# A spectral stage's causal filters computed in two block levels with three products each, image by image

## The chip, the core and the metric

The kernel is one program on one core of a Trainium2 chip. The core's engines are TensorE (PE, matrix products from SBUF into PSUM), VectorE (DVE), ScalarE (ACT), GpSimd (POOL) and SyncE (SP), which issues the DMAs. Each engine runs its own instruction list; semaphores order them. The metric is the device time of one execution in microseconds; three runs of the kernel before gave 12062.67 to 12078.81, median 12070.78.

## The reference

A four-layer model on x of 2 images x 4096 tokens x 128 channels, float32. The change touches one part, the spectral feed-forward of layer 2:

```python
for i, frac in enumerate((1, 2, 4, 8)):
    xi = x[:, :T // frac]
    si = _stu(xi, sigma, phi, M_u[i], M_phi_plus[i], M_phi_minus[i])   # padded back to T tokens
    outs.append(si)
# _stu: for each of K = 16 filters phi[:, k] (4096 taps, causal):
#   U_plus  = conv(phi_k, u);  U_minus = sgn * conv(phi_k, sgn * u),  sgn = +1, -1, +1, ...
#   out += sigma_k**0.25 * (U_plus @ M_phi_plus[k] + U_minus @ M_phi_minus[k])
#   out += three-tap autoregressive term with M_u
return jnp.sum(stacked * weights, axis=-1)    # weights: hard Gumbel choice over the four ranges
```

As the filters are causal, one convolution serves all four ranges; the ranges differ only in the matrices, which are summed beforehand for the tokens that belong to them. U_plus and U_minus are sum and difference of the convolutions of the even and the odd tokens, so the kernel works with two half-length sequences (2048 tokens each, "parities") and with M_plus + M_minus and M_plus - M_minus.

## The kernel before

Stages follow one another; each has its own tiles, semaphores and instruction lists, and ends with its stores to HBM landed. Two stages matter here.

**Preparation** (`spectral_prepare`). SP loads x, the normed x, and small tables. TensorE transposes xn into tokens by channels (L1837), reverses the order in each block with an exchange matrix (L1843), and computes the three-tap term (L1854); VectorE copies the results out (L1900, L1903) and adds the third to y (L1907). A short chain of VectorE gives the 16 x 4 scales. SP stores u, the scales and y to HBM.

**Spectral stage** (`spectral`). SP loads u; VectorE splits it into a high part (rounded to float32r) and the rest (L2042, L2044). For each of 16 filters the loop runs over both images and eight output chunks of 256 positions. A convolution job `conv(n)` is one chunk of one input parity: for each block j of 128 input tokens up to the chunk's end, three products (high x high, low table x high u, high table x low u, L2001) of a 128x128 block of u with a Toeplitz window of the filter, 2 x 256 columns (both output parities). Chunk c has 2c + 2 blocks; the last block covers only half of the columns (a 256-column matmul). So an image, filter and parity takes 36 pairs of chunks, each of two halves, each of three matmuls. ScalarE copies a finished bank to the high part (L2032), VectorE takes the low part (L2078), then `mix(i)` multiplies both by the matrices of the filter, six matmuls (L2012), and VectorE adds them to y (L2085). Convolution banks are four, mixing banks two; `mix(i - 1)` is queued behind the two jobs of chunk i.

The Toeplitz table is a filter with a one-element shift per partition. SP loads it in 16 pieces of 128 KB (L1969), VectorE splits each (L2052, L2054) between the chunks of the filter before, and combines the 16 matrices' sum, difference and ranges (`combine`, L2063 to L2074) at the filter's end. The order in each engine's list is that of the code; TensorE, ScalarE, VectorE and SP run it in loops on the engine (`Fori`).

## Time and profile before

| | us |
|---|---|
| median of three runs | 12070.78 |
| the profiled execution: its own time | 12065.87 |
| its span, first to last instruction | 12064.1 |
| TensorE busy (matmul) | 10848.0, 90% |
| VectorE / ScalarE / GpSimd busy | 6660.2 / 5168.2 / 5561.0 |
| mean granted TensorE clock | 0.946 |

The matmul records overlap, since a matmul starts before the one ahead of it is through; a busy TensorE is therefore not a TensorE at its peak, and a matmul's share of time is read from start to start. The idle time in a row is that of the engine just before the instruction, with what ended it. In the DMA views, "us to landing" counts from issue to the completion that the semaphore shows.

### The profile page before, as it was taken

Reading aid. Unit: us, or ns where it says so; the run is one execution under the profiler, and the core shown is the slowest. Engines: PE = TensorE matmul, PEld = TensorE weight load, DVE = VectorE, ACT = ScalarE, POOL = GpSimd, SP = SyncE. Lnnn points to the kernel's source line nnn. Section 1 sums busy time; section 2 is a strip of 40 time slices with the busy share of each in tenths; the row PEclk is TensorE's granted clock in tenths of the full one; section 3 lists DMA queues with packets and bytes.
Section 4 is the critical chain, followed back from the end, with each engine's and each line's share of the span. In section 5 each row is a group of like instructions: output and inputs, shape, how many; then the busy total and the mean of one; then the engine's idle time right before and its main releaser. Section 6 shows DMA issues by size and latency. Waiting matters only on the chain. (4 is left out here: it accounts for less than half of the span.)

```text
span 12064.1 us, 153269 instructions
## 1 busy us (share of the span) xinstructions
PE 10848.0 (90%) x48496; PEld 8411.9 (70%) x48496; DVE 6660.2 (55%) x7766; ACT 5168.2 (43%) x13553; POOL 5561.0 (46%) x2940
## 2 busy tenths in 40 slices
PE   7999999999776999999953999959999999999977
PEld 5677666777435888888841665638878888887854
DVE  6677766777556999999964433332222222222226
ACT  5788777877546777777720222200000000000000
POOL 4778777877536999999940364600000000000000
PEclk9999999999877999999976899979999999999988
DMA  2111111111245444444433000030000000000021
GB/s 75 29 37 39 37 38 28 39 38 30 84 177 182 107 108 106 106 108 105 107 126 122 28 9 13 9 127 11 13 14 12 14 12 12 14 12 14 8 88 73
DMA packets 509926, 697.55 MB, mean 58 GB/s; under 512 B 277816, under 2 KB 323008, under 8 KB 496064
## 3 DMA queue, kind: packets, MB, share of 16 engines
q1 hardware_dynamic: 509248, 688.60, 19.7%
q8 instruction: 415, 6.80, 0.2%
q14 instruction: 263, 2.15, 0.1%
HBM read 415.96 MB, written 190.62 MB: 50 GB/s over the span
## 5 line engine op out<-in xcount | busy, mean ns | idle before, releaser
L687 POOL TENSOR_TENSOR l_probs_low<-l_probs,l_probs_high 128x512 fp32r<-128x512 f32 x1792 | 2384.5, 1360 | 798.8 <-ACT l_probs_high L657 784.6
L1388 POOL TENSOR_TENSOR m_c_h<-m_h,m_c 128x2048 f32<-128x2048 f32 x520 | 2341.2, 4562 | 44.3 <-DVE m_h L1375 44.2
L1375 DVE TENSOR_TENSOR_SCAN m_h<-m_decay,m_ps_x 128x1024 f32<-128x1024 f32 x1040 | 2270.4, 2262 | 91.3 <-issue 62.8
L1288 PE MATMUL m_ps_y<-m_c_h,m_ident 128*128 128x256 f32 x8320 | 1977.0, 381 | 2.1 <-POOL m_c_h L1388 2.1
L2001 PE MATMUL s_ps_all<-s_toeplitz_high,s_u_high 128*128 128x512 f32 (+1 forms) x4608 | 1782.9, 387 | 106.3 <-DVE s_toeplitz_low L2054 101.2
L2078 DVE TENSOR_TENSOR s_filtered_low<-s_ps_all,s_filtered_high 128x512 fp32r<-128x512 f32 x512 | 351.0, 690 | 2674.7 <-ACT s_filtered_high L2032 2663.9
L2001 PE MATMUL s_ps_all<-s_toeplitz_low,s_u_high 128*128 128x512 f32 (+1 forms) x4608 | 1774.0, 385 | 0.0
L2001 PE MATMUL s_ps_all<-s_toeplitz_high,s_u_low 128*128 128x512 f32 (+1 forms) x4608 | 1769.1, 384 | 0.0
L2032 ACT ACTIVATE s_filtered_high<-s_ps_all 128x512 fp32r<-128x512 f32 x512 | 306.2, 598 | 3313.4 <-PE s_ps_all L2001 3313.4
L743 DVE TENSOR_REDUCE l_max_by_row<-l_ps_all 128x8 f32<-128x512 f32 x2048 | 1357.9, 685 | 529.1 <-PE l_ps_all L506 446.8
L1288 PEld LDWEIGHTS m_ps_y<-m_c_h,m_ident 128*128 128x128 f32 x8320 | 1509.0, 190 | 174.3 <-POOL m_c_h L1388 3.6
L655 ACT ACTIVATE l_probs<-l_ps_all 128x512 f32<-128x512 f32 x2048 | 1239.1, 605 | 455.6 <-PE l_ps_all L547 308.3
L657 ACT ACTIVATE l_probs_high<-l_ps_all 128x512 fp32r<-128x512 f32 x2048 | 1234.8, 603 | 0.0
L2001 PEld LDWEIGHTS s_ps_all<-s_toeplitz_high,s_u_high 128*128 128x128 f32 x4608 | 872.1, 189 | 308.6 <-issue 113.5
L2001 PEld LDWEIGHTS s_ps_all<-s_toeplitz_high,s_u_low 128*128 128x128 f32 x4608 | 874.3, 190 | 197.0
L2001 PEld LDWEIGHTS s_ps_all<-s_toeplitz_low,s_u_high 128*128 128x128 f32 x4608 | 869.5, 189 | 194.0
L1312 ACT ACTIVATE m_b_diagonals<-m_steps,m_b_rows 128x32 fp32r<-128x32 f32 x4160 | 966.8, 306 | 3.2 <-DMA m_b_rows<-b_t 3.1
L1278 PE MATMUL m_ps_x<-m_b_diagonals,m_delta_u 128*128 128x256 f32 x4160 | 858.3, 329 | 68.2 <-issue 34.3
L557 PE MATMUL l_ps_all<-l_probs_high,l_v_parts 128*128 128x512 f32 x2048 | 847.2, 414 | 6.0 <-POOL l_probs_low L687 5.5
L558 PE MATMUL l_ps_all<-l_probs_low,l_v_parts 128*128 128x512 f32 x2048 | 809.9, 395 | 0.0
L547 PE MATMUL l_ps_all<-l_q_and_row_bias,l_k_low_and_cell 128*128 128x512 f32 x2016 | 801.3, 397 | 0.0
L1726 POOL TENSOR_TENSOR l_probs_sum<-l_probs_sum,l_probs 128x512 f32<-128x512 f32 x480 | 615.1, 1281 | 357.4 <-ACT l_probs L1710 355.1
(293 smaller groups left out, 15113.8 us busy)
## 6 DMA issues: line engine op xcount, KB each, us to landing
m_delta_u<-du_t SPq DMA_DIRECT2D x1040, 128.0 KB, 3.7
m_c<-c_windows SPq DMA_DIRECT2D x130, 512.0 KB, 4.2
l_q_and_row_bias<-l_q_parts SPq DMA_DIRECT2D x64, 512.0 KB, 5.1
du_t<-m_delta_u_high SPq DMA_DIRECT2D x128, 256.0 KB, 3.0
du_t<-m_delta_u_low SPq DMA_DIRECT2D x128, 256.0 KB, 3.0
m_direction<-ys SPq DMA_DIRECT2D x16, 2048.0 KB, 9.3
ys<-m_y SPq DMA_DIRECT2D x256, 126.0 KB, 4.8
s_toeplitz<-in_phi SPq DMA_DIRECT2D x240, 128.0 KB, 2.9
```

Of the source, the lines that this page charges most:

```text
L557: pe.matmul(o, vv[:, i, :], ph[:, i % SLOTS, :], start=(i == 0), stop=False)
L558: pe.matmul(o, vv[:, i, :], pl[:, i % SLOTS, :], start=False, stop=(i == KT - 1)).then_inc(weighed, 1)
L655: act.activation(pt[:, i % SLOTS, :], ps[:, i % 3, :], ACT.Exp)
L657: act.activation(ph[:, i % SLOTS, :], ps[:, i % 3, :], ACT.Exp).then_inc(expd, 1)
L687: pool.tensor_tensor(pl[:, slot, :], pt[:, slot, :], f(ph[:, slot, :]), ALU.subtract).then_inc(low_pool, 1)
L743: dve.tensor_reduce(dst, ps[:, MAX0 + u % 2, :].rearrange("p (x y) -> p x y", y=SIDE), AX.X, ALU.max).then_inc(max_taken, 1)
L1278: ins = pe.matmul(x_ps[:, step % X, bank * TW:(bank + 1) * TW].rearrange("p (n t) -> p n t", t=SPAN)[:, :, half * HALF:(half + 1) * HALF], ...
L1288: ins = pe.matmul(y_ps[:, group % 2, 0:DIRS * SPAN].rearrange("p (d t) -> p d t", d=DIRS), ident[:, :], ch[:, group % CH, :, n, :], start= ...
L1312: ins = act.activation(diag[:, span % 2, k, n * HALF:(n + 1) * HALF], ones[:, :], ACT.Copy, scale=rows[:, group % 2, k, span % ROW_SETS, n ...
L1375: dve.tensor_tensor_scan(h[:, u % H, :], decay[:, pair % 2, ct, k % 2, :, :].rearrange("p n t -> p (n t)"), x_ps[:, u % X, :], 0.0, ALU.mu ...
L1388: pool.tensor_tensor(ch[:, group % CH, 2 * pair % DIRS:2 * pair % DIRS + 2, :, :].rearrange("p d n t -> p d (n t)"), h[:, 2 * pair % H:2 * ...
L2001: ins = pe.matmul(o, uu[:, at_u], both, start=(j == 0 and q == 0), stop=(j == last and q == 2))
```

## The change

The eight chunks of the output are computed in pairs by a three-product scheme at two levels. With b(c) the chunk c, T(j) a filter's Toeplitz block at a distance of j chunks, and u(c) an input chunk, the pair (2, 3) needs T(2)u0 + T(1)u1 + T(0)u2 and T(3)u0 + T(2)u1 + T(1)u2 + T(0)u3. The product T(2)(u0 - u1) is shared: added to (T(1) + T(2))u1 it gives the even chunk's part, taken from (T(2) + T(3))u0 the odd chunk's. The same is done once more with chunks taken two at a time. The terms table says for each job which filter family (raw, near sums, far sums, sums of both), distance j and input chunk it uses; chunks 8 to 13 of u are differences.

The preparation stage now also makes the four filter families and splits them, makes the six differences of each image, splits all 14 u chunks (high part on ScalarE, low part on GpSimd), and combines and splits the 16 filters' matrices on VectorE, one behind each of its 16 sums; all go to HBM. The spectral stage loads ready tables. The image is the outermost loop: 32 passes of one image and one filter, each written out with no loop on the engine, 28 jobs over six banks. y holds one image, is stored and loaded anew after pass 15.

Core of the diff (the first part is in `spectral_prepare`):

```diff
+            for n in range(PIECES):
+                b, c = n // U_CHUNKS, n % U_CHUNKS
+                sp.wait_ge(u_high_ok, n + 1)
+                sp.dma_start(u_parts[0, b, :, c, :, :], uh[:, n % 4, :, :].bitcast(F32)).then_inc(u_high_stored[n % 4], 16)
+                sp.wait_ge(u_low_ok, n + 1)
+                sp.dma_start(u_parts[1, b, :, c, :, :], ul[:, n % 4, :, :].bitcast(F32)).then_inc(u_low_stored[n % 4], 16)
+                if n % 2 and n // 2 < K - 1:
+                    sp.wait_ge(m_used, 2 * (n // 2) + 2)
+                    sp.dma_start(mraw[:, :, :], m_phi[(n // 2 + 1) * P:(n // 2 + 2) * P, :]).then_inc(m_in, 16)
+                    matrix(n // 2)
...
             for t in range(NT):
                 dve.wait_ge(turned, t + 1)
                 dve.tensor_copy(ut[:, t * TW:(t + 1) * TW], tr_ps[:, t % 4, :]).then_inc(copied, 1)
+                if t % 4 == 3:
+                    f = t // 4
+                    dve.wait_ge(filter_high_ok, f + 1)
+                    if f:
+                        dve.wait_ge(filter_low_stored, 16 * f)
...
+                    dve.tensor_tensor(fl[:, :], (taps, near, far, far)[f][:, 0:FILTER_LEN], fh[:, :].bitcast(F32), ALU.subtract).then_inc(filter_low_ok, 1)
...
+                if k:
+                    dve.wait_ge(m_stored, 16 * k)
+                dve.tensor_copy(parts[:, :, 0, :, :], meff[:, :, :, :]).then_inc(m_ok, 1)
+                dve.wait_ge(m_ok, 2 * k + 1)
+                dve.tensor_tensor(parts[:, :, 1, :, :], meff[:, :, :, :], parts[:, :, 0, :, :].bitcast(F32), ALU.subtract).then_inc(m_ok, 1)
...
             for t in range(NT):
                 dve.wait_ge(auto, t + 1)
                 part = y[:, t * TW:(t + 1) * TW]
                 dve.tensor_tensor(part, ar_ps[:, t % 2, :], part, ALU.add).then_inc(added, 1)
+                combine(t)
+                if t == 5:
+                    differ_far(0)
+                if t == 12:
+                    differ_far(1)
```

In `spectral`, the jobs of a pass, their terms as (family, distance, input chunk), and what is queued where:

```diff
+    jobs = [("b0", 0), ("b1", 0), ("b0", 1), ("b1", 1)]
+    for s in range(2):
+        jobs += [("q", s), ("b2", s), ("b3", s)]
+    for s in range(2):
+        jobs += [("i", s), ("g", s), ("h", s)]
+    for s in range(2):
+        jobs += [("e", s), ("b4", s), ("b5", s)]
+    for s in range(2):
+        jobs += [("f", s), ("b6", s), ("b7", s)]
...
+    terms = {
+        "b0": [(RAW, 0, 0)], "b1": [(RAW, 1, 0), (RAW, 0, 1)],
+        "q": [(RAW, 2, 8)], "b2": [(RAW, 0, 2), (NEAR, 1, 1)], "b3": [(RAW, 1, 2), (RAW, 0, 3), (NEAR, 2, 0)],
+        "i": [(RAW, 4, 13)], "g": [(NEAR, 3, 12)], "h": [(NEAR, 4, 11)],
+        "e": [(FAR, 2, 9)], "b4": [(RAW, 0, 4), (FAR_NEAR, 1, 3)], "b5": [(RAW, 1, 4), (RAW, 0, 5), (FAR_NEAR, 2, 2)],
+        "f": [(FAR, 4, 8), (RAW, 2, 10)], "b6": [(RAW, 0, 6), (NEAR, 1, 5), (FAR_NEAR, 3, 1)],
+        "b7": [(RAW, 1, 6), (RAW, 0, 7), (NEAR, 2, 4), (FAR_NEAR, 4, 0)],
+    }
...
+            for i in range(PASSES):
+                for job in jobs:
+                    if job == ("b0", 1) and i:
+                        mix(i - 1, 6)
+                        mix(i - 1, 7)
+                    for c, after in ((0, ("q", 1)), (2, ("i", 1)), (4, ("f", 1))):
+                        if job == after:
+                            mix(i, c)
+                            mix(i, c + 1)
+                    conv(i, job)
...
+            for i in range(PASSES):
+                for s in range(2):
+                    low(i, 0, s)
+                    low(i, 1, s)
+                    if s == 0 and i:
+                        add(i - 1, 6)
+                        add(i - 1, 7)
+                near_rows(i, 0)
+                add(i, 0)
+                add(i, 1)
+                near_rows(i, 1)
+                crossing(i, 0)
+                add(i, 2)
+                add(i, 3)
+                crossing(i, 1)
+                for s in range(2):
+                    far_rows(i, 4, s)
+                far_rows(i, 6, 0)
+                add(i, 4)
+                add(i, 5)
+                far_rows(i, 6, 1)
```

`near_rows` adds a shared product (copied out of its bank by ScalarE, tile `common`) to two banks, `crossing` does this for the far pair into the tile `cross`, `far_rows` makes four operations of two banks; each then takes two low parts from the tile `rows`. The first pass's loads, and what the later passes wait for on SP:

```diff
+                if i == 0:
+                    load_u(0, 0)
+                    load_always(0)
+                    for c in (1, 8, 2, 3):
+                        load_u(0, c)
+                    for r in range(RANGES):
+                        load_matrices(0, r)
+                    for n, cs in enumerate(((13,), (12, 11), (9,), (4, 5), (), (6, 10, 7))):
+                        for c in cs:
+                            load_u(0, c)
+                        load_single(0, n)
+                    load_y(0)
...
+                    for n in range(6):
+                        sp.wait_ge(convolved, done_at(i, last_use[n]))
+                        load_single(i + 1, n)
+                        if k == K - 1:
+                            for c in ((13,), (12, 11), (9,), (2, 3), (8, 10), (0, 1, 4, 5, 6, 7))[n]:
+                                load_u(b + 1, c)
...
+                    if k == K - 1:
+                        sp.wait_ge(added, 8 * (i + 1))
+                        sp.dma_start(y_out[:, b * L:(b + 1) * L], y[:, :]).then_inc(stored, 16)
+                        sp.wait_ge(stored, 16 * (b + 1))
+                        load_y(b + 1)
```

TensorE's list at the start of the spectral stage, what stood there (128x2x128 is a short matmul):

```order
L1979 UNCONDITIONAL_BRANCH
L1979 ISA
L1990 ISA
L2001 MATMUL s_ps_all<-s_toeplitz_high,s_u_high 128x512
L2001 MATMUL s_ps_all<-s_toeplitz_low,s_u_high 128x512
L2001 MATMUL s_ps_all<-s_toeplitz_high,s_u_low 128x512
L2001 MATMUL s_ps_all<-s_toeplitz_high,s_u_high 128x2x128
```

and now (x2 stands for two equal rows, here the high and the low part of the table):

```order
L2190 UNCONDITIONAL_BRANCH
L2239 MATMUL s_ps_all<-s_toeplitz,s_u_high 128x512 x2
L2239 MATMUL s_ps_all<-s_toeplitz,s_u_low 128x512
L2239 MATMUL s_ps_all<-s_toeplitz,s_u_high 128x2x128 x2
L2239 MATMUL s_ps_all<-s_toeplitz,s_u_low 128x2x128
```

The engine loop is gone, and behind chunk 0's six matmuls comes chunk 1 of the same parity, not chunk 0 of the other.

VectorE's list in the preparation stage, behind the scales, before:

```order
L1892 TENSOR_SCALAR s_m_range<-s_m_u,s_scales 128x384
L1894 SCALAR_TENSOR_TENSOR s_m_range<-s_m_u,s_scales,s_m_range 128x384 x3
L1900 COPY s_u_tok<-s_ps_turned 128x512 x16
L1903 COPY s_u_tok<-s_ps_auto 128x512 x16
L1907 TENSOR_TENSOR s_y<-s_ps_auto,s_y 128x512 x16
```

and now, from the last of four groups of copies to the second sum:

```order
L1973 COPY s_u_tok<-s_ps_turned 128x512 x4
L1981 TENSOR_TENSOR s_filter_low<-s_far_sums,s_filter_high 32x1536
L1987 COPY s_u_tok<-s_ps_auto 128x512 x16
L1993 TENSOR_TENSOR s_differences<-s_u_tok 128x512 x6
L2025 TENSOR_TENSOR s_y<-s_ps_auto,s_y 128x512
L2008 TENSOR_TENSOR s_sum_and_difference<-s_m_phi 128x4x128
L2009 TENSOR_TENSOR s_sum_and_difference<-s_m_phi 128x4x128
L2011 TENSOR_SCALAR s_m_ranges<-s_sum_and_difference,s_scales 128x256
L2013 SCALAR_TENSOR_TENSOR s_m_ranges<-s_sum_and_difference,s_scales,s_m_ranges 128x256 x3
L2016 CAST s_m_parts<-s_m_ranges 128x4x256
L2018 TENSOR_TENSOR s_m_parts<-s_m_ranges,s_m_parts 128x4x256
```

Between the copies stand the filters' low parts, and between the sums the work on one filter's matrices that stood at L2063 to L2074.

SP's list in the spectral stage, before, up to the first of a filter's 16 pieces (one pass of the loop), and in a pass now, from its third table load to its eighth:

```order
L1962 DMA s_y<-y 128x8192
L1963 UNCONDITIONAL_BRANCH
L1963 ISA
L1969 ISA
L1969 DMA s_toeplitz<-in_phi 128x256
L1967 REGISTER_ALU
```

and now:

```order
L2125 DMA s_toeplitz<-filters 128x2x770
L2125 DMA s_toeplitz<-filters 128x2x642
L2138 DMA s_m_parts<-matrices 128x512 x2
L2125 DMA s_toeplitz_sums<-filters 128x2x386 x2
L2125 DMA s_toeplitz_sums<-filters 128x2x642 x2
```

One filter's loads for both images were 16 pieces and one matrix block; now each pass has 16 table loads, of 386 to 770 columns twice, and four of matrices.

## Rows read from the trace of the kernel before

**Rows 1.** Stages: busy us and count by engine, granted clock, DMA share, GB/s.
```profile
core 0: us, PE busy (x) PEld busy (x) DVE busy (x) ACT busy (x) POOL busy (x), PEclk, DMA share, GB/s
...
8041.00:8053.00 12.00, 0.00 (x0) 0.00 (x0) 0.00 (x0) 0.00 (x0) 0.00 (x0) 0.54 0.82 350
...
8335.00:8552.00 217.00, 215.05 (x960) 174.06 (x960) 48.02 (x90) 19.13 (x32) 0.00 (x0) 1.00 0.06 13
```

**Rows 2.** Groups by shape, spectral stage: busy us, mean ns, idle before, releaser.
```profile
L2001 PE MATMUL s_ps_all<-s_toeplitz_high,s_u_high 128*128 128x512 f32 x4096 | 1637.2, 400 | 106.3 <-DVE s_toeplitz_low L2054 101.2 <-issue 5.1
...
L2078 DVE TENSOR_TENSOR s_filtered_low<-s_ps_all,s_filtered_high 128x512 fp32r<-128x512 f32 x512 | 351.0, 690 | 2674.7 <-ACT s_filtered_high L2032 2663.9 <-issue 10.8
L2032 ACT ACTIVATE s_filtered_high<-s_ps_all 128x512 fp32r<-128x512 f32 x512 | 306.2, 598 | 3313.4 <-PE s_ps_all L2001 3313.4
...
L2001 PE MATMUL s_ps_all<-s_toeplitz_high,s_u_low 128*128 128x256 f32 x512 | 146.8, 287 | 0.0
```

**Rows 3.** Timeline, TensorE, late in the spectral stage: start us, us, instruction.
```profile
11561.24 0.40 PE L2001 MATMUL s_ps_all<-s_toeplitz_high,s_u_high 128*128 128x512 f32 x1
...
11568.24 0.40 PE L2001 MATMUL s_ps_all<-s_toeplitz_high,s_u_high 128*128 128x512 f32 x1
```

**Rows 4.** Timeline, TensorE, end of the spectral stage.
```profile
11583.02 0.28 PE L2001 MATMUL s_ps_all<-s_toeplitz_high,s_u_low 128*128 128x256 f32 x1
11583.14 0.40 PE L2012 MATMUL s_ps_all<-s_filtered_high,s_m_high 128*128 128x512 f32 x1
...
11584.79 0.49 PE L2012 MATMUL s_ps_all<-s_filtered_high,s_m_high 128*128 128x512 f32 x1
...
11586.04 0.40 PE L2012 MATMUL s_ps_all<-s_filtered_low,s_m_high 128*128 128x512 f32 x1
```

**Rows 5.** Timeline, SyncE queue and TensorE, start of the spectral stage.
```profile
8053.09 0.32 SPq L1957 DMA_DIRECT2D s_scales<-scales  x1
...
8117.80 0.79 PE L2001 MATMUL s_ps_all<-s_toeplitz_high,s_u_high 128*128 128x512 f32 x1 [78.03 <-DVE s_toeplitz_low L2054]
```

**Rows 6.** Timeline, TensorE, first matmul of the third filter, with idle before.
```profile
8552.59 0.49 PE L2001 MATMUL s_ps_all<-s_toeplitz_high,s_u_high 128*128 128x512 f32 x1 [2.18 <-DVE s_toeplitz_low L2054]
```

**Rows 7.** Stage table, 10 us around that matmul.
```profile
8551.00:8561.00 10.00, 8.41 (x34) 6.97 (x35) 7.75 (x15) 1.79 (x3) 0.00 (x0) 0.83 0.16 30
```

**Rows 8.** Stage table, 700 us of the scan stage of layer 1.
```profile
4200.00:4900.00 700.00, 693.07 (x3739) 623.14 (x3738) 679.29 (x312) 531.27 (x2249) 698.50 (x156) 1.00 0.42 107
```

**Rows 9.** DMA queues, 8130 to 11300 us: packets, MB, share of 16 engines.
```profile
q1 hardware_dynamic: 35856, 38.17, 5.3%
```

**Rows 10.** DMA throughput in 40 slices of 8075 to 8118 us.
```profile
GB/s 488 30 457 488 488 488 488 457 366 167 229 1 26 90 129 0 69 140 35 20 78 122 24 27 103 96 18 67 83 70 25 84 55 85 55 80 64 54 262 337
```

**Rows 11.** DMA issues, 7900 to 11650 us: count, KB each, median us to landing.
```profile
s_toeplitz<-in_phi SPq DMA_DIRECT2D x240, 128.0 KB, 2.9
...
xn<-ln_centred SPq DMA_DIRECT2D x7, 1024.0 KB, 3.9
...
s_y<-u_tok SPq DMA_DIRECT2D x2, 2048.0 KB, 9.6
```

**Rows 12.** Timeline, preparation, and VectorE at the spectral stage's start.
```profile
7969.60 3.67 DVE L1900 COPY s_u_tok<-s_ps_turned 128x512 f32<-128x512 f32 x6
...
7998.29 41.47 PE L1854 MATMUL s_ps_auto<-s_xn,s_m_range 128*128 128x512 f32 x96 [0.78 <-DVE s_u_tok L1903]
...
8040.52 0.32 SPq L1824 DMA_DIRECT2D y<-s_y  x1
...
8063.25 4.43 DVE L2044 TENSOR_TENSOR s_u_low<-s_y,s_u_high 128x4096 fp32r<-128x4096 f32 x1
...
8118.37 0.69 DVE L2064 TENSOR_TENSOR s_sum_and_difference<-s_m_phi 128x512 f32<-128x512 f32 x1
...
8122.37 1.23 DVE L2074 TENSOR_TENSOR s_m_low<-s_m_range,s_m_high 128x1024 fp32r<-128x1024 f32 x1
```

**Rows 13.** The page's costliest groups: the low parts that GpSimd makes in attention.
```profile
L687 POOL TENSOR_TENSOR l_probs_low<-l_probs,l_probs_high 128x512 fp32r<-128x512 f32 x1792 | 2384.5, 1360 | 798.8 <-ACT l_probs_high L657 784.6
```

More of the change, by code:

```diff
@@ L1946, in f, with two, places, bank @@
             return ap.bitcast(F32)
[L1948 to L1953 removed]
+        def two(ap):
+            return ap.rearrange("p (kind t) -> p kind t", t=CW)
+        def places(tile, c, s):
+            return tile[:, c % 2, 0:4:3, :] if s == 0 else tile[:, c % 2, 1:3, :]
+        def bank(i, job):
+            return ps[:, (i * PER_PASS + place[job]) % BANKS, :]
@@ L1955, in _, with done_at @@
+        def done_at(i, job):
+            return i * PER_PASS + place[job] + 1
         @block.sync
         def _(sp):
[L1957 to L1971 removed]
```

513 lines of the change are left out of this document (338 added, 175 removed).

## The prediction

> **What bounds the kernel now.** I read first the stage table (busy time in chosen stretches) [rows 1], to find which part of the 12064 us the change touches: the preparation stage, which ends at 8053 us, and the spectral stage behind it. The reader is to see that in the spectral stage TensorE is busy 215 of every 217 us at full granted clock, VectorE 48, ScalarE 19, and the DMA engines 6%. Then the groups by shape [rows 2]: 3 x 4096 full convolution matmuls and 3 x 512 short ones (256 columns), beside the 1536 mixing matmuls that the code has; VectorE's idle time ends with ScalarE and ScalarE's with TensorE, not the other way round. Their mean durations (about 400 ns) overlap, so the time of a matmul is read from start to start [rows 3]: from 11561.24 to 11568.24 lie 30 slots, 0.2333 us each; a short one takes 0.12 [rows 4]. One filter and one image is then 432 full and 48 short slots, 100.8 + 5.8 = 106.6 us, and 32 of them 3411. The stage runs from 8117.8 to 11586.4 [rows 4, 5], 3468.6 us, so 58 are gaps. After each filter TensorE waits for the last table piece of the next, here 2.2 us [rows 6], and behind this one the granted clock over 10 us is 0.83 [rows 7], which is 3.4 us at 1.2 instead of 2.4 GHz, 1.7 us lost.
>
> **Spectral stage, TensorE.** The pairs (output chunk, input chunk) of one image, filter and parity fall from 36 to 27 (count the terms table: 1+2+1+2+3 for the first four chunks and their common product, 3 for i, g, h, then 1+2+3 and 2+3+4). Each pair is 2 halves x 3 products, and there are 2 x 32 of them: 36-27 = 9, 9 x 6 x 64 = 3456 full matmuls fewer. The short ones and the mixing stay. 3456 x 0.2333 = 806 us. The pass of one image and filter becomes 324 full + 48 short = 75.6 + 5.8 = 81.4 us, 32 of them 2605.
> The 58 us of gaps: the tables are now loaded ready split, double-buffered or a pass ahead, so the wait at each filter's end has nothing to wait for. I keep 3 us for the slow slots at the stage's start (they are in both) and take 55 back. If nothing came back, the time is 55 longer.
>
> **Is the cover there?** What TensorE needs in a pass is VectorE's and ScalarE's. VectorE gets 24 row and cross operations beside 16 low parts and 8 sums: 48 x 0.69 = 33 us; ScalarE 20 x 0.60 = 12; both far under 81. The order matters more. In [rows 4] the chain from the last convolution matmul through ScalarE and VectorE to the mixing matmul takes 1.8 us (11583.02 to 11584.79). Walking the job list with 1.40 us a term (1.06 for the one with a short half): chunk 7's last bank is done at T; its row sum, the low part of 6 and that of 7 end at T+1.0, T+1.7 and T+2.4; the mixes of 6 and 7 stand at T+3.5 and T+4.9, behind two jobs of the next pass. For chunks 2 and 3 low parts end 2.4 us after b3, and the mix stands 4.2 us after it. For chunks 4 and 5 it stands behind f, b6 and b7 (11.9 us). A bank comes round after six jobs; the closest is b0's, whose low part ends 6.5 us into the pass (ScalarE waits for the mix of 6) and which b3 wants at 13.6. So no wait of TensorE is forecast; the least slack is 1.8 us, at the mixes of 6, 2 and 3. TensorE's code is no longer a loop (order rows of the change); a long straight stretch exists in the trace, 3739 matmuls in 700 us with DMA at 42% and TensorE 99% busy [rows 8], so I charge nothing for fetching.
>
> **Its DMAs.** A pass loads tables of 4 x (788 or 657 KB) and 12 x (395 or 657 KB), 9.2 MB, and 1.05 MB of matrices, all on SP: 10.3 MB in 81.4 us, 126 GB/s. Before, 38.2 MB took 5.3% of 3170 us [rows 9], which is 227 GB/s when busy, with 1 KB rows mostly; the new rows are 1.5 to 3 KB. At 227 a pass needs 45 us of its 81. Each table is asked for right after its last use and needed 57 to 72 us later. Hidden; the cover ends at 126 GB/s.
>
> **Start of the stage.** Before: 64.7 us from the first issue to the first matmul (8053.09 to 8117.80) [rows 5], for loading u, splitting it, and 16 table pieces. After: 0.5 MB of u and 2.9 MB of tables. The price of such loads lies between 227 GB/s and the 488 at which y streamed [rows 10]; I take 300, since the rows are two to three times as long as at 227 but not 16 KB. 3.4/300 = 11.4, plus 2 to the first landing and 2.6 of issues: 16 us. Gain 49 (47 to 53).
> Then y0 is the last of the first pass's loads: 7.3 + 9.2 + 1.05 + 2.1 = 19.7 MB, landed at 68 us (42 at 488, 89 at 227). VectorE meets it at its first sum, about 41 us; behind that wait stand the rows of chunks 2 and 3, for which TensorE waits from its 51st us. It goes on 4.2 us after y: 68 + 4 - 51 = 21, and 3 for slow slots: +24 (0 to 45).
> The Trainium skill, "DMA: Bandwidth & Descriptors", section Specifications, gives a core about 358 GB/s of HBM; here a load showed 488, so the trace disagrees. By 358 y would land at 57 us and the time come out 11 us lower.
>
> **Change of image** (once): at the end of pass 15 the last table part (1.3 MB) and u's first chunks (1 MB) can only be asked for then: 2 + 2.3/300 = 10 us of waiting, 2 for slow slots. Storing and reloading y (2 MB landed in 9.6) [rows 11] takes about 18 from the last sum, and is reached by VectorE at nearly the same time. +12 (9 to 25).
> **End**: y's store is 2 MB in place of 4; 4 MB took the 12 us of an otherwise empty stretch at 350 GB/s [rows 1], so half of the bytes saves 5 to 6: -5.
>
> **Preparation.** Loads grow by 0.8 MB: +2. VectorE gets near and far (2048 and 1536 elements; 4096 took 4.43 [rows 12], so 2.2 and 1.7): +4. Between the 16 copies stand four low parts of 1.7 and one more sum; three of the low parts wait for the store before, 3 us from issue: copies and flips, 28.7 us from 7969.60 to 7998.29, become some 36: +7. The flips stay as they are.
> Then VectorE did 16 sums under TensorE's 2.57 us apiece: 7998.3 to 8040.5, 42 us. Now every sum is followed by a combine, whose rows are 12 too: 8118.37 to 8123.6 is 5.2 us. That was hidden under convolutions before; here it is the path. 5.9 us a turn is the floor. The parts tile has one buffer: its copy waits for the store of 1 MB that went out after the turn before. 1 MB landed in 3.9 us [rows 11], plus 0.4 of issue and 1.9 for copy and low part: 6.2. But each turn also moves 1 MB of u parts and 0.5 MB of matrices on the same queue, 2.6 MB, which at 350 GB/s (the store in rows 1) is 7.5 us. I take 7.2 for 15 turns: 108, the first 5.9, the six differences 3.7, the far differences 3: 121, that is +79; the last matrix store ahead of y0 adds 2.5. The nearest slower row, 9.6 us for 2 MB, makes a turn 11.5 and +65; the floor makes it -19. GpSimd's 28 low parts (1.36 each [rows 13]) run under this. Sum of the preparation: 2 + 4 + 7 + 81.5 = +94 (75 to 159).
>
> **Sum**, against the profiled execution's 12065.87 (span 12064.1; 5 us under the median of the runs, 12070.78): -806 -55 -49 +24 +12 -5 +94 = -785, so **11281 us**.
>
> **Rivals.**
> (a) The chain is late. Each pair of mixes waits out one such chain, 1.8 us, since every row now passes bank, row tile, ScalarE and VectorE. 4 x 1.8 x 32 = 230: 11510. For it: VectorE's order is fixed, and it often waits for a later matmul before an older low part. Against it: the walk above. 0.11.
> (b) The loads follow each other without overlap. A 128 KB load landed in 2.9 us [rows 11], 0.6 of it data: 2.3 x 20 + 45 = 91 us a pass, 10 over: +320, 11600. Against it: two loads of 2 MB in one 488 GB/s stream. 0.06.
> (c) Slower than before: TensorE loses its clock. Its jobs are now 6 to 24 matmuls with a bank hand-over after each, and a wait of some 2 us can bring 1.2 GHz [rows 6, 7]. At that clock throughout (512 columns in 0.427 us) a pass is 324 x 0.427 + 48 x 0.213 = 149 us, 67 more: +2150, 13430. It decides from 785/32 = 25 us a pass, 36% of the stage at the low clock, or six such waits a pass of 2.2 us with 1.7 lost behind each. "TensorE: Matmul & The Clock Gate", section A second HAM failure mode, in the Trainium skill, says just this of kernels that cycle through PSUM banks: short idle stretches between groups make the clock swing. By that rule the change would lose; the trace of before cycles four banks and keeps 1.00 in most stretches, which speaks against it. 0.03.
> (d) No change, because the added preparation or an exposed DMA eats everything: it needs 790 us, eight times the preparation's cost. 0.01.
> Forecast: 0.79.
>
> **Range and chances.** Around the forecast: preparation -19 to +65, y -24 to +21, gaps not returned +55, stage start and image +15; slots longer by 1% under ten times the DMA traffic, +26. Not all fall together: 11225 to 11400 for the likeliest case. Taking in (a)'s near half gives 11220 to 11440 for 8 in 10. 0.2% is 24 us, about what a measurement can tell from no change. Faster 0.96, within 0.2% 0.01, slower 0.03.
>
> **What would show it.** Convolution matmuls 10368; a pass of 81 us with 0.233 slots and granted clock 1.00; TensorE waiting for nothing at mixes; DMA share near 0.5 in the stage; VectorE about 40% busy. First matmul 16 us after the first issue, one wait of some 20 us in the first pass and one of 10 at the middle. Preparation some 94 us longer, with VectorE's copy to the parts tile ended by the DMA of the matrix store. The forecast is wrong if TensorE's rows name VectorE, ScalarE or a DMA before them in every pass, or if slots stand at 0.25 or more.

## The result and the profile after

The changed kernel takes 11302.08 us (median of 4 runs, 11294.99 to 11319.06) against 12066.73 for the kernel before in the same session: ratio 0.9367, 95% interval 0.9351 to 0.9383. The prediction was 11281 (11225 to 11400 for its likeliest case). The profiled execution has a span of 11295.0 us against 12064.1.

Stage table of the changed kernel (columns as in [rows 1]): the stop in the first pass, the second pass to its end, and 400 us further on.

```profile
8213.00:8232.00 19.00, 0.16 (x2) 0.11 (x1) 3.36 (x6) 1.54 (x3) 0.00 (x0) 0.58 1.01 361
8320.00:8401.40 81.40, 81.40 (x374) 66.83 (x373) 31.69 (x48) 12.46 (x21) 0.00 (x0) 1.00 0.51 127
8800.00:9200.00 400.00, 400.00 (x1830) 328.36 (x1829) 156.15 (x237) 60.67 (x98) 0.00 (x0) 1.00 0.55 128
```

A pass is 81.4 us in which TensorE is busy all the time at full granted clock, VectorE 31.7 and ScalarE 12.5; the DMA engines moved 127 GB/s at a share near one half. In [rows 1] TensorE stood still 2 us in 217 (of 217.00 us it was busy 215.05). The groups by shape, which answer to [rows 2]:

```profile
L2239 PE MATMUL s_ps_all<-s_toeplitz,s_u_high 128*128 128x512 f32 x3584 | 1134.0, 397 | 59.4 <-DMA s_toeplitz<-filters 50.3 <-DMA s_u_low<-u_parts 9.2
...
L2239 PE MATMUL s_ps_all<-s_toeplitz_sums,s_u_high 128*128 128x512 f32 x2304 | 722.5, 394 | 0.0
L2239 PE MATMUL s_ps_all<-s_toeplitz,s_u_low 128*128 128x512 f32 x1792 | 709.6, 396 | 0.0
L2239 PE MATMUL s_ps_all<-s_toeplitz_sums,s_u_low 128*128 128x512 f32 x1152 | 455.4, 395 | 0.0
...
L2315 DVE TENSOR_TENSOR s_filtered_low<-s_rows,s_filtered_high 128x512 fp32r<-128x512 f32 x384 | 264.4, 689 | 144.3 <-ACT s_filtered_high L2293 131.3
```

The four conv groups give 3584 + 2304 + 1792 + 1152 = 8832 full matmuls in place of 12288; with the 1536 short ones they are the 10368 of the prediction. Idle time of TensorE is named only at the stage's start and at three places. The waits of TensorE between first and last matmul (columns: us in total, times, longest):

```profile
PE s_ps_all L2250 <- DVE s_filtered_low L2315: 18.8, 1, 18.8
PE s_ps_all L2239 <- DMA s_u_low<-u_parts: 9.2, 1, 9.2
PE s_ps_all L2250 <- issue: 1.5, 1, 1.5
```

The first is y in the first pass, the second the change of image, the third the last pair of mixes, with no further jobs behind them to cover the chain. The timeline of TensorE around the stage (the first row answers to [rows 5], the fourth to the end in [rows 4]):

```profile
8181.64 1.22 PE L2239 MATMUL s_ps_all<-s_toeplitz,s_u_high 128*128 128x512 f32 x2 [50.25 <-DMA s_toeplitz<-filters]
...
8231.92 1.19 PE L2250 MATMUL s_ps_all<-s_filtered_high,s_m_parts 128*128 128x512 f32 x2 [18.84 <-DVE s_filtered_low L2315]
...
9513.37 1.19 PE L2239 MATMUL s_ps_all<-s_toeplitz,s_u_high 128*128 128x512 f32 x2 [9.18 <-DMA s_u_low<-u_parts]
...
10821.19 0.39 PE L2250 MATMUL s_ps_all<-s_filtered_low,s_m_parts 128*128 128x512 f32 x1
...
10837.21 3.75 PE L217 MATMUL ln_ps_mean<-ln_x,ln_channel_mean 128*128 128x512 f32 x4 [15.63 <-DMA ln_x<-x]
```

From 8181.64 to 10821.58 are 2639.9 us, before 3468.6.

The preparation. Rows of the timeline of SyncE's queue and VectorE, answering to [rows 12]:

```profile
7938.26 0.33 SPq L1837 DMA_DIRECT2D s_ident<-in_ident  x1
...
7966.66 0.16 DVE L1945 TENSOR_TENSOR s_logits<-s_logits,s_gumbel 128x4 f32<-128x4 f32 x1 [28.25 <-DMA s_y<-x]
...
7967.18 2.27 DVE L1948 TENSOR_TENSOR s_near_sums<-s_taps 32x2048 f32<-32x2048 f32 x1
...
7976.18 2.48 DVE L1973 COPY s_u_tok<-s_ps_turned 128x512 f32<-128x512 f32 x4
...
8012.65 8.07 DVE L1993 TENSOR_TENSOR s_differences<-s_u_tok 128x512 f32<-128x512 f32 x6
...
8020.64 0.68 DVE L2025 TENSOR_TENSOR s_y<-s_ps_auto,s_y 128x512 f32<-128x512 f32 x1
...
8131.62 0.69 DVE L2008 TENSOR_TENSOR s_sum_and_difference<-s_m_phi 128x512 f32<-128x512 f32 x1 [5.37 <-DMA s_m_phi<-in_m_phi]
...
8147.77 1.23 DVE L2018 TENSOR_TENSOR s_m_parts<-s_m_ranges,s_m_parts 128x1024 fp32r<-128x1024 f32 x1
...
8165.61 0.32 SPq L2142 DMA_DIRECT2D s_u_high<-u_parts  x1
```

From the first issue at 7938.26 to the next stage's at 8165.61 are 227.4 us, before 116.4 (7936.67 to 8053.09). VectorE's waits for transfers from 8015 to 8150 us:

```profile
DVE s_sum_and_difference L2008 <- DMA s_m_phi<-in_m_phi: 24.4, 12, 5.4
...
DVE s_m_parts L2016 <- DMA matrices<-s_m_parts: 0.7, 3, 0.3
```

### The profile page after: what moved, and what is told of

It is laid out like the page before. It is cut to its first block and busy times, and to the rows that moved or that the text cites. A ratio compares the mean times of both kernels' runs of the same rounds, so it can differ in the third digit from the quotient of the medians.

```text
span 11295.0 us, 145513 instructions
## 1 busy us (share of the span) xinstructions
PE 10041.4 (89%) x45040; PEld 7767.0 (69%) x45040; DVE 7000.2 (62%) x8021; ACT 5281.4 (47%) x13713; POOL 5607.0 (50%) x2968
## 5 line engine op out<-in xcount | busy, mean ns | idle before, releaser
L2239 PE MATMUL s_ps_all<-s_toeplitz,s_u_high 128*128 128x512 f32 (+1 forms) x4608 | 1327.8, 372 | 59.4 <-DMA s_toeplitz<-filters 50.3
L2293 ACT ACTIVATE s_filtered_high<-s_rows 128x512 fp32r<-128x512 f32 x384 | 242.8, 632 | 1765.9 <-DVE s_rows L2366 899.1
L2239 PEld LDWEIGHTS s_ps_all<-s_toeplitz,s_u_high 128*128 128x128 f32 x4608 | 845.8, 189 | 240.1 <-DMA s_toeplitz<-filters 51.4
L2239 PE MATMUL s_ps_all<-s_toeplitz,s_u_low 128*128 128x512 f32 (+1 forms) x2304 | 855.9, 371 | 0.0
L506 PE MATMUL l_ps_all<-l_k_high_and_column,l_q_and_column_bias 128*128 128x512 f32 x1792 | 733.8, 416 | 43.5 <-issue 24.1
L546 PE MATMUL l_ps_all<-l_q_and_column_bias,l_k_high_and_column 128*128 128x512 f32 x1792 | 729.3, 407 | 34.3 <-DMA l_q_and_row_bias<-l_row_bias_low 32.7
L1278 PEld LDWEIGHTS m_ps_x<-m_b_diagonals,m_delta_u 128*128 128x128 f32 x4160 | 642.2, 191 | 135.2 <-issue 74.8
L2239 PE MATMUL s_ps_all<-s_toeplitz_sums,s_u_high 128*128 128x512 f32 x2304 | 722.5, 394 | 0.0
```

The lines of the kernel that those rows point to most:

```text
L1278: ins = pe.matmul(x_ps[:, step % X, bank * TW:(bank + 1) * TW].rearrange("p (n t) -> p n t", t=SPAN)[:, :, half * HALF:(half + 1) * HALF], ...
L2239: ins = pe.matmul(o, uu[:, c, s, half * P:(half + 1) * P], both, start=(n == 0 and q == 0), stop=(n == len(work) - 1 and q == 2))
```

## The experiments

In each, the stage's times are read from its own trace, one trace a kernel. The part of the program ahead of the preparation varies: its first issue comes between 7928.1 us (experiment 9) and 7945.0 us (the second run of experiment 7), so small effects are read from the stage and not from the total. The preparation varies too: in the five traces in which its code is that of the changed kernel (the change, experiments 1, 4, 8 and 9) it takes 225.2 to 230.0 us, and its stretch from the first sum to the last low part 126.3 to 129.3. An effect on it counts where it lies outside these bounds.

**1. The removed matmuls put back.**

```diff
-work = [(family, j, c, half) for family, j, c in terms[name] for half in range(2)]
+doubled = {"b1": 1, "b2": 1, "b3": 1, "b4": 1, "b5": 1, "b6": 2, "b7": 2}.get(name, 0)
+work = [(family, j, c, half) for family, j, c in terms[name] + terms[name][-1:] * doubled for half in range(2)]
```

> The changed kernel with nine of its 27 products of chunks per pass and parity done twice (the last term of b1 to b5 once more, that of b6 and b7 twice more), so that a pass has the old 432 full matmuls; its sums are not the reference's. Theory A (the gain is the count of matmuls): 3456 x 0.2333 = 806 us come back, the pass grows from 81.4 to 106.6 us, total 11302 + 806 = 12108. That is above the kernel before by about 41, which is what the preparation costs (+111) less what the gaps and the start give (-55 and -49, of which the first pass's wait takes 24 and the change of image 12 back). Theory B (a good part of the gain is the new order of loads and banks, and the removed matmuls were worth less than a slot each): total under 12000.

Measured: 12076.55 us, ratio to the kernel before 1.0003 (0.9994 to 1.0012). The last term of b1 has a short half, which the expectation overlooked: 3264 full and 192 short matmuls came back, not 3456 full. 3264 x 0.2333 + 192 x 0.12 = 784.5. The waits show that the stop for y shrank, since the longer pass reaches it later:

```profile
PE s_ps_all L2251 <- DVE s_filtered_low L2316: 9.6, 1, 9.6
```

784.5 - (18.8 - 9.6) = 775.3; the stage grew from 2639.9 to 3414.6, by 774.7. Theory A holds to 1 us.

**2. The removal alone, on the old structure.** Left out are the second and later input blocks of each output chunk, 1, 1, 1, 2, 2, 2 chunks' worth for chunks 2 to 7.

```diff
+dropped = 2 * (0, 0, 1, 1, 1, 2, 2, 2)[c]
 for j in range(last + 1):
+    if 1 <= j <= dropped:
+        continue
```

> The kernel before with one in four of its convolution terms left out (output chunks 2, 3, 4 lose one pair of chunks each, 5, 6, 7 lose two, wait: 1, 1, 1, 2, 2, 2 for chunks 2 to 7), its tables still split by VectorE under the convolutions; its sums are not the reference's. Theory A (count alone): the filter falls from 213.2 to 162.8 us of matmuls, VectorE with 48 of 217 us stays far under it, so 3456 x 0.2333 = 806 us go: 12067 - 806 = 11261, and the gaps at the filters' ends stay at about 58. Theory B (the split of the next filter's tables, one piece per pair of banks, was hidden only by the long filters): the first chunks of each image are short, pieces come late, and each filter waits more than 2.2 us: total over 11300.

Measured: 11260.32 us, ratio 0.9323 (0.9308 to 0.9337), 807 us less. TensorE's waits behind the first filter:

```profile
PE s_ps_all L2004 <- DVE s_toeplitz_low L2057: 17.1, 10, 2.2
PE s_ps_all L2004 <- issue: 10.3, 4, 2.6
```

Theory A: VectorE splits the tables in time even at 2657.0 / 16 = 166 us a filter, and no wait is longer than before. The stage fell by 811.6 us to 2657.0, only 17 more than in the changed kernel. So this stage's gain is the count of matmuls: beyond the 2605 of its slots this kernel has 52 us of gaps, and the changed one 35, of which 28 are the two stops. What the changed kernel pays for being allowed to drop them is the difference of the totals, 42 us.

**3. The last table piece of the kernel before, split earlier.**

```diff
-                        if not last:
-                            split(k + 1, 1 - s, i - 1)
+                        for piece in {8: (7, 8), 11: (11, 12), 15: (), 9: (9,), 10: (10,), 12: (13,), 13: (14,), 14: (15,)}.get(i, (i - 1,)):
+                            if not last:
+                                split(k + 1, 1 - s, piece)
                 add(k, YJOBS - 1)
                 if not last:
-                    split(k + 1, 1 - s, PIECES - 1)
```

> The kernel before with the last table pieces of the next filter split one to two sums earlier (two pieces behind the eighth and the eleventh sum, none behind the last), nothing else. Theory A (the gaps at the filters' ends are waits for the last table piece): 15 times 2.2 us of waiting and 1.7 us of low clock go, total 12067 - 58 = 12010, at most -35 if only the waits go. Theory B (the wait behind it, for the bank that VectorE frees or for the matrices, ends at nearly the same time): within 15 us of 12067.

Measured: 12063.1 us, ratio 0.9995 (0.9986 to 1.0004): not to be told from no change. The waits of TensorE in the stage, first of the kernel before, then of this one:

```profile
PE s_ps_all L2001 <- DVE s_toeplitz_low L2054: 23.1, 13, 2.4
PE s_ps_all L2001 <- issue: 5.1, 2, 2.6
```

```profile
PE s_ps_all L2001 <- issue: 16.7, 7, 2.5
PE s_ps_all L2012 <- DVE s_filtered_low L2078: 1.7, 8, 0.2
```

The waits for the table piece are gone, as theory A says, and the stage is 15.2 us shorter (3453.5). But at seven places TensorE now stops for 2.4 us while it waits for nothing that the trace shows. They lie 431 to 433 us apart, where its loop of two filters turns:

```profile
8548.94 0.50 PE L2001 MATMUL s_ps_all<-s_toeplitz_high,s_u_high 128*128 128x512 f32 x1 [2.54 <-issue]
```

Seven of the 15 waits had covered this stop. Neither theory had it. That it is the loop's turn is inferred from the place and from the changed kernel, whose TensorE code is no loop and which has no such stop; a kernel before with its loop written out was not run.

**4. y earlier in the first pass.**

```diff
                     for r in range(RANGES):
                         load_matrices(0, r)
+                    load_y(0)
                     ...
-                    load_y(0)
```

> The changed kernel with the load of y for the first image moved ahead of the later input chunks and sum tables of the first pass, behind its matrices. Theory A (the stop of 18.8 us in the first pass is y being the last of 20 MB): the stop goes, total 11302 - 19 = 11283, or 11280 with the slow slots behind it. Theory B (at 350 GB/s the loads of the first pass are late anyway; y taken ahead only moves the stop to the tables of chunks 4 to 7): the stop comes back behind it as waits for tables of up to 6 us each, total 11290 to 11302.

Measured: 11282.67 us, ratio 0.9341 (0.9329 to 0.9354). Stage 2620.7 us, 19.2 less; all that TensorE waits for in it:

```profile
PE s_ps_all L2239 <- DMA s_u_low<-u_parts: 9.2, 1, 9.2
PE s_ps_all L2250 <- issue: 1.5, 1, 1.5
```

Theory A. The tables behind y were not late.

**5. Two buffers for the raw matrices**, the load of k + 2 issued where that of k + 1 was.

```diff
-sp.dma_start(mraw[:, :, :], m_phi[(n // 2 + 1) * P:(n // 2 + 2) * P, :])
+sp.dma_start(raw(n // 2), m_phi[(n // 2 + 2) * P:(n // 2 + 3) * P, :])
```

> The changed kernel with two buffers for the raw mode matrices in the preparation, so that each is asked for a turn earlier. Theory A (each turn waits for this load, 24.4 us in all, as the trace of the changed kernel shows): the waits go, a turn falls from 7.6-8.0 to about 6.4 us, total 11302 - 20 = 11282 (-15 to -25). Theory B (the queue's bytes set the turn, 2.6 MB at 350 GB/s = 7.5 us): the wait moves to the store of the matrix parts, total -0 to -8, 11294 to 11302.

Measured: 11292.47 us, ratio 0.9358 (0.9345 to 0.9370), its interval overlapping that of the change; preparation 225.8 us against 227.4, which is inside its variation. The stretch from the first sum to the last low part, 123.8 us, is 2.5 below the shortest of the unchanged ones. The stage table of 8020 to 8145 us, of the changed kernel and of this one, and this one's VectorE waits:

```profile
8020.00:8145.00 125.00, 61.38 (x84) 22.12 (x84) 96.68 (x146) 13.70 (x22) 37.09 (x25) 0.72 0.79 294
```

```profile
8020.00:8145.00 125.00, 61.07 (x83) 21.13 (x81) 109.34 (x148) 13.70 (x22) 37.09 (x23) 0.69 0.81 304
```

```profile
DVE s_m_parts L2022 <- DMA matrices<-s_m_parts: 9.0, 11, 2.3
```

The wait of 24.4 us for the raw load is gone. Of it 9.0 came back as the wait for the store of the parts, and VectorE's busy time rose from 96.7 to 109.3 for the same kind of work: theory B in size and, for 9.0 us, in its wait; the slower work is a second cause that neither theory had (experiment 7).

**6. Two buffers for the split matrices** (the second in the tile of the near sums, which is free by then).

```diff
-if k:
-    dve.wait_ge(m_stored, 16 * k)
+if k >= 2:
+    dve.wait_ge(m_stored[k % 2], 16 * (k // 2))
```

> The changed kernel with two buffers for the split matrices in the preparation, so that the copy into them no longer waits for the store of the turn before. Theory A (the prediction's: this store sets the turn): a turn falls from 8 to 6, total 11302 - 25 = 11277. Theory B (as the trace of the changed kernel shows, 0.7 us of waiting for this store in all; the raw load sets the turn): no change, 11300 +- 4.

Measured: 11307.46 us, ratio 0.9368 (0.9355 to 0.9381); preparation 228.7. Theory B: the store of the parts was not what a turn waited for. But the preparation's inside did change, which the total hides: the stretch from the first sum to the last low part fell from 128.4 to 123.7 us, while that from the last low part to the next stage grew from 16.6 to 22.4. VectorE ran ahead, and the stores that it no longer waited for still had to land at the end.

**7. GpSimd taken out of the preparation**, with one raw buffer and with two.

```diff
-pool.tensor_tensor(ul[:, n % 4, :, :], piece(n), uh[:, n % 4, :, :].bitcast(F32), ALU.subtract)
+act.activation(ul[:, n % 4, :, :], piece(n), ACT.Copy)
```

> The changed kernel with the preparation's 28 subtractions on GpSimd left out; ScalarE writes a second copy of the high part in place of each low part, so that every byte still moves (the input's low parts are then not the reference's). In the traces so far VectorE's operations with two SBUF inputs took 1.55 to 1.77 us when GpSimd's ran beside them and 0.69 when not. Theory A (this contention is the missing part of the preparation): the six differences fall from 8.1 to 4.2 us, the turns by 0.3 us each on average: preparation 227 to about 218, total 11302 - 9 = 11293. Theory B (the bytes of the queue set the turns, GpSimd only fills waiting time): only the differences are quicker, total 11298 to 11302.

> Both: GpSimd's subtractions left out as in the run before, and two buffers for the raw matrices. With two buffers alone the waits for the raw load went (24.4 us to none) but VectorE's busy time in the same 125 us rose from 96.7 to 109.3, so the turns gained 4.5 us only. Theory A (load wait and GpSimd's contention hide each other): a turn comes down to VectorE's own 6.0 to 6.4 us, first sum to last low part 128 -> 103, preparation 227 -> 199, total 11302 - 28 = 11274. Theory B (bytes: 2.6 MB a turn at 294 to 350 GB/s is 7.5 to 8.8 us): the turns stay above 7.3, first sum to last low part at least 118, total 11290 or more.

Measured: 11289.12 us (0.9351, 0.9336 to 0.9365) and 11283.5 us (0.9347, 0.9332 to 0.9361); both intervals overlap that of the change. Preparation 217.4 and 211.9 us, both far outside its variation. The second's waits of VectorE:

```profile
DVE s_m_parts L2017 <- DMA matrices<-s_m_parts: 21.7, 15, 3.7
```

The contention itself stands in the timeline of the changed kernel, VectorE beside GpSimd and alone, then GpSimd's own row. The last row is of the kernel before: VectorE's share of the low parts in attention, with the shortest, median and longest duration in ns, in a part where GpSimd made the others [rows 13]:

```profile
8021.24 1.18 DVE L2008 TENSOR_TENSOR s_sum_and_difference<-s_m_phi 128x512 f32<-128x512 f32 x1
...
8022.34 1.76 DVE L2009 TENSOR_TENSOR s_sum_and_difference<-s_m_phi 128x512 f32<-128x512 f32 x1
...
8111.16 0.69 DVE L2008 TENSOR_TENSOR s_sum_and_difference<-s_m_phi 128x512 f32<-128x512 f32 x1 [1.91 <-DMA s_m_phi<-in_m_phi]
...
8111.77 0.68 DVE L2009 TENSOR_TENSOR s_sum_and_difference<-s_m_phi 128x512 f32<-128x512 f32 x1
...
8013.35 10.20 POOL L1937 TENSOR_TENSOR s_u_low<-s_u_tok,s_u_high 128x512 fp32r<-128x512 f32 x6 [151.21 <-ACT s_u_high L1929]
...
L765 DVE TENSOR_TENSOR l_probs_low<-l_probs,l_probs_high x256: 668/1777/1794, 155.1 to 3177.6; 128x512 fp32r<-128x512 f32 x128
```

GpSimd runs from 8013.35 to 8023.55. In that time an operation of VectorE with two inputs from SBUF takes up to 1.78 us in place of 0.68 (four of the six differences 1.75 to 1.78, the two rows above 1.18 and 1.76); the sum into y (line 2025), whose one input comes from PSUM, takes its 0.68 all the same. The Trainium skill, "SBUF — State Buffer", section Who interferes with whom, says that a two-input operation of VectorE with both inputs in SBUF contends with GpSimd's reads; the trace agrees, and the prediction had left that rule out. The trace of before had its price as well: the row of line 765 is the same operation on the same shape, 1.78 us in the median and 0.67 at its shortest. With one raw buffer the differences take 3.7 us in place of 8.1 and the stretch from the first sum to the last low part falls from 128.4 to 121.4: theory A. With two buffers as well it falls to 117.1 (123.8 with two buffers alone). The second run lies between its two theories: 211.9 us does not reach the 199 of theory A, and the 21.7 us of waiting for the store of the parts say that the queue decides next, as theory B has it. (117.1 - 3 - 6) / 15 = 7.2 us a turn is the number that the prediction took, but in a kernel with a second raw buffer and GpSimd idle. In the first run, the nearest to what was priced, a turn is (121.4 - 3 - 6) / 15 = 7.5. One thing was not separated: ScalarE now writes both copies of a piece, so the pieces' pace changed together with GpSimd's absence.

**8. The mixes brought forward.**

```diff
-if job == ("b0", 1) and i:
+if job == ("b0", 0) and i:
     mix(i - 1, 6)
     mix(i - 1, 7)
-for c, after in ((0, ("q", 1)), (2, ("i", 1)), (4, ("f", 1))):
+for c, after in ((0, ("q", 1)), (2, ("g", 0)), (4, ("f", 1))):
```

> The changed kernel with the mixes of chunks 2, 3 (two jobs earlier, ahead of g instead of i) and 6, 7 (two jobs earlier, ahead of the next pass's first) moved towards their low parts. The walk of the prediction gives these mixes 1.8 us of slack. Theory A (the walk is right): two jobs are 2.8 us, of which 1.8 are covered for chunks 2 and 3: 1.0 us of waiting per pass there; for 6 and 7 the mix stands right behind the last job, so its wait is the whole chain of about 2.4 us and a second for 7: 1.0 + 2.4 = 3.4 us a pass, 32 x 3.4 = +109, total 11410. Theory B (the slack is larger, since VectorE takes rows ahead): total within 40 of 11302. Theory C (gaps lower the clock as well, as at the filters' ends of the kernel before, 1.7 us lost for each gap of 2.2): total 11410 + 32 x 1.7 = 11465 or more.

Measured: 11357.41 us, ratio 0.9411 (0.9397 to 0.9426); stage 2704.9, +65. Between A and B. TensorE's waits:

```profile
PE s_ps_all L2250 <- issue: 48.3, 32, 1.8
PE s_ps_all L2250 <- DVE s_filtered_low L2315: 21.3, 1, 21.3
```

All 32 waits, 31 of 1.5 us and one of 1.8, are at the mix of chunk 6, none above half a microsecond at chunk 2. From start to start such a mix stands 1.89 us behind the matmul before it, where a slot is 0.23: 32 x 1.66 = 53 of the 65 us (one of them the changed kernel has too). The rest is the balance of stops of 0.1 to 0.2 us at the mix of chunk 2 and between mixes, 2.5 more at the stop for y and 4.6 less at the change of image. Theory C falls: with a wait in every pass the granted clock stays at 1.00.

```profile
8800.00:9200.00 400.00, 393.93 (x1788) 320.40 (x1787) 151.79 (x231) 58.27 (x94) 0.00 (x0) 1.00 0.50 120
```

Low part and mix in the changed kernel, one pass's end:

```profile
8609.67 1.48 DVE L2315 TENSOR_TENSOR s_filtered_low<-s_rows,s_filtered_high 128x512 fp32r<-128x512 f32 x2
...
8612.33 0.63 PE L2250 MATMUL s_ps_all<-s_filtered_high,s_m_parts 128*128 128x512 f32 x2
```

The row holds the low parts of 6 and 7, 0.69 us each; the first ends at 8610.36 and its mix starts at 8612.33: 2.0 us of slack (1.8 in the prediction's walk). The two jobs of b0 and b1 that now come after it are 3.5 us: 3.5 - 2.0 = 1.5. My mistake in the expectation was to let the first mix wait for both low parts; it needs one, and the second is ready when its turn comes. At chunk 2 the slack was 2.7, and two jobs are 2.8. So the cover of the chain is real but thin: rival (a) of the prediction needed the chain only 2 us later.

**9. More load on the DMA engines.** A second stream on GpSimd's queue, 16 loads a pass into a tile that nothing reads.

```diff
+pool.wait_ge(sunk, 16 * (16 * i + n))
+pool.dma_start(sink[:, :, :], src).then_inc(sunk, 16)
```

> The changed kernel with 16 more table loads of 395 KB in every pass, issued one behind the other on GpSimd's queue into a tile that nobody reads: 6.3 MB a pass more, 205 GB/s instead of 127. Theory A (loads are hidden while the share of the DMA engines stays under one): the stage stays 2640 us, total 11302 +- 10, with the share going from 0.52 to about 0.85. Theory B (table loads are on the edge: each is needed 57 to 72 us after it can be asked for): TensorE waits for tables in each pass, 2 to 10 us, total 11370 to 11620.

Measured: 11965.6 us, ratio 0.9917 (0.9902 to 0.9932), and that total doesn't answer the question: the loads wait for one another, 512 of them took 6.5 us each, and 673 us of them were left when the stage's last matmul ended. The 186 GB/s that follow are then not the 205 that the expectation aimed at. Inside the stage (2643.5 us against 2639.9) the table says:

```profile
8720.00:9120.00 400.00, 400.00 (x1832) 328.37 (x1831) 155.82 (x237) 61.27 (x99) 41.19 (x57) 1.00 0.78 186
```

Theory A: at 186 GB/s and a share of 0.78 TensorE still waits for no table. Of the 3.6 us, 2.8 are the two stops, which are 1.0 and 1.8 longer.

**10. A version meant to beat both**: y early (4), two raw buffers (5), the differences finished before ScalarE and GpSimd begin on the pieces, the loads that the weights need first and x last, and two of the 16 combinations done while the large input loads.

```diff
+for dst, src in ((z, logits_in), (g4, gumbel_in), (sg, sigma_in), (rank, rank_in)):
+    sp.dma_start(dst[:], src).then_inc(small, 16)
...
+for k in range(EARLY):
+    combine(k)
+dve.wait_ge(loaded, LOADS)
...
+act.wait_ge(differed, 6)
```

> A version meant to beat both. The changed kernel with: y of the first image loaded early in the spectral stage (-19, measured); in the preparation two raw matrix buffers (-4.5 measured in the turns), the six differences finished before ScalarE and GpSimd start on the pieces (-4), x loaded behind and apart from the loads that the first operations need (4 of 9 MB, -8 to -11), and the weights of the modes and two of the 16 combinations done while the large input still loads (two turns of 8 us become sums of 2.6, -11; softmax and scales beside the load, -5). Sum -52 to -55, total about 11249. If the bytes set the preparation (some 50 MB at 300 GB/s = 167 us, against 182 us now between landing and last store), it ends at -35, total 11267. If the early stores and loads hold up the input's load: -25, 11277.

Measured: 11262.22 us (11251.69 to 11272.39), ratio to the kernel before 0.9331 (0.9318 to 0.9344); 40 us under the changed kernel. The stage is 2618.7 us, 2 less than with y early alone, and the preparation 208.7 instead of 227.4 (its first issue is now that of the logits, at 7932.08 us). That is 19 less, where 33 to 36 had been expected. The stage table, columns as above:

```profile
8020.00:8145.00 125.00, 49.44 (x69) 17.78 (x67) 98.56 (x131) 13.87 (x22) 36.30 (x22) 0.66 0.85 318
```

318 GB/s at a share of 0.85, and VectorE busy 98.6 us though two combinations fewer fall in it. That looks like both limits of experiment 7 at once; which of the version's parts gave less than expected was not tested, since all were put in together.

## Why the prediction was right, and where it was off

The time fell inside the range, 21 us above the point, and the mechanism was the forecast one: the removed matmuls are the gain, experiments 1 and 2 show it from both sides. The misses partly cancel: the preparation came out 17 us dearer and the gaps gave back 4 less, the two stops cost 8 less. By its steps:

- **Matmuls, -806.** Right: experiment 1 gives back 774.7 us where its own count makes 775.3, experiment 2 takes 807 from the total (812 from the stage) on the old structure.
- **Gaps, -55.** The stage lost 828.7 us; less 806 for the matmuls and plus 18.8 and 9.2 for the two stops, that leaves -50.7 for the gaps and slow slots. Right in sum, and in part by luck. The prediction read one filter end [rows 6, 7], 2.2 us of waiting and 1.7 lost at 1.2 GHz behind it; fifteen of them are just its 58 us. Two filter ends of the kernel before, the first and the second (columns as in [rows 1]):

```profile
8335.00:8345.00 10.00, 9.74 (x47) 8.17 (x48) 8.50 (x16) 2.40 (x4) 0.00 (x0) 1.00 0.13 21
8552.00:8562.00 10.00, 9.41 (x40) 7.84 (x41) 6.98 (x12) 2.36 (x4) 0.00 (x0) 0.83 0.11 24
```

The granted clock fell behind seven of the 15 waits only, the seven at the turns of the loop, where from start to start 2.5 to 3.0 us pass in place of 1.9. Read from start to start, the 58 us are some 31 of waiting, 14 of low clock and some 14 in slots a little longer than 0.2333, which the changed kernel does not have; what lengthened them is open. And the step "the wait at each filter's end has nothing to wait for" took the last releaser for the only one: behind it stood a stop of TensorE's own, by its place that of the loop (experiment 3). The changed kernel has neither.
- **Start, -49**: 16.0 us from first issue to first matmul, -48.7. **End, -5**: -3.9. **Change of image, +12**: 9.2 of waiting (10 taken, and 2 for slow slots).
- **y in the first pass, +24 (0 to 45)**: 18.8 (21 taken, and 3 for slow slots), and experiment 4 gives 19.2 back.
- **No other wait** of TensorE, and least slack 1.8 us at the mixes: measured none, and 2.0 (experiment 8). Rivals (a) and (c) did not come: the granted clock is 1.00 but for the start, the two stops and 3 to 5 us behind each (0.58 in the first one's row). Rival (b), loads without overlap, falls by the pass itself, 81.4 us without a wait for a table; experiment 9 shows room beyond it.
- **Preparation, +94: measured +110.9.** This is the mis-sized term. The first issue to the first operation of VectorE grew by 2.7 (2 taken); near and far sums, 2.3 net (4); copies and flips 36.5 (36). Three steps missed: the six differences took 8.1 and not 3.7 (+4.4), the 16 turns with the far differences 128.4 and not 117 (+11.4), and the last low part to the next stage 16.6 and not 15.1 (+1.5).
- The step that failed is the one that priced VectorE's rows as they ran alone in [rows 12] and added the queue's time beside them as a rival bound. With GpSimd beside it VectorE's rows are up to 2.6 times as long (experiment 7). The trace of before had no such row for these operations, but it had one for the same operation on the same shape (line 765), in the same stage as the GpSimd row from which the prediction took its 1.36 us [rows 13]. Without GpSimd the preparation is 10.0 us shorter, 4.4 of them in the differences; that the predicted 7.2 us a turn comes back only when a second raw buffer is added is a coincidence of numbers. And **the wait was named wrongly**: "its copy waits for the store of 1 MB" is 0.7 us in the trace, the raw load 24.4. On SyncE's queue the raw load stands behind four stores of pieces, and each turn asked for it only when its one buffer was free. Experiment 6 shows that this store held up no turn, the second run of experiment 7 that it is the next wait.

What stays open: the second run of experiment 7 still takes 117.1 us for what VectorE alone could do in 16 x 6.0 + 3 = 99. How much of the 18 is the queue's order and how much its bandwidth was not separated; that experiment 6 moved 5 us from the turns to the end without a gain speaks for the queue as a whole.

## What to carry to other kernels

Where one engine is busy all the time at one clock, removed instructions are worth their slot to a per cent, and the risk sits in what the scheme must prepare: price the preparation as a stage of its own, with every engine that will run in it, since rows read from a stage in which a neighbour was idle are too short, and look in the trace for the same operation beside that neighbour. When a wait is to be removed, look for what ends just behind it: one more buffer turned 24 us of waiting into 9 of another wait and 13 of slower work. A wait priced from one place and multiplied wants a second place read: here every other one behaved differently. A cover of 2 us in a pass of 81 holds, if it is counted from the one result that the waiting instruction needs.

## What the runs showed of the hardware

- VectorE beside GpSimd: 0.68 to 0.69 us alone, up to 1.78 us beside it for 128x512 float32 from two SBUF inputs, though not each time (of the five differences that ran beside it one kept 0.68, and so did the two of line 2001, 0.69); no change with an input from PSUM (0.68). A cast with one input, 0.69 us elsewhere, took this once beside it:

```profile
8083.24 1.81 DVE L2016 CAST s_m_parts<-s_m_ranges 128x1024 fp32r<-128x1024 f32 x1
```
- TensorE's granted clock stayed at 1.00 behind waits of 1.5 us in every pass (experiment 8), but for the one of 1.8. It fell to 1.2 GHz for some 3.4 us behind the seven longer of the 15 waits of the kernel before, and behind three of the seven stops of 2.4 us in experiment 3.
- An issue on SyncE's queue costs up to four times as much (0.32 and 1.27 us below) when others stand before it. Rows of the changed kernel's preparation, close behind other stores and after a pause:

```profile
8051.62 1.27 SPq L1855 DMA_DIRECT2D u_parts<-s_u_high  x1
...
8052.93 1.16 SPq L1857 DMA_DIRECT2D u_parts<-s_u_low  x1
...
8065.98 0.32 SPq L1855 DMA_DIRECT2D u_parts<-s_u_high  x1
```
- The Trainium skill, "DMA: Bandwidth & Descriptors", section Specifications, has about 358 GB/s of HBM for a core. The loads of the first pass, mostly tables with rows of 1.5 to 3 KB and then y, ran at 361 GB/s over 19 us with the share at 1.01, so in this mean the trace agrees with it. It does not in shorter stretches: slices of the same loads show up to 458, and where [rows 10] shows 488, the mean of 8075 to 8085 us is 419.
